# Surplus branches nested, down weights loaded in another order and into two rooms, GpSimd's transfers and subtractions reordered in a routed feed-forward kernel

## The reference

```python
x = x + tanh(g_xattn[0]) * xattn(layernorm(x), ctx, Wq, bq, Wk, bk, Wv, bv)
# xattn: softmax((q Wq + bq)(ctx Wk + bk)^T) / 16 @ (ctx Wv + bv)
x = x + tanh(g_ffn[0]) * ffn(layernorm(x), router_w, gate_w, up_w, down_w)
# ffn: e = argmax(h @ router_w.T) for each token;
#      y = (silu(h @ gate_w[e].T) * (h @ up_w[e].T)) @ down_w[e].T
```

## Time and profile before

| | us |
|---|---|
| median of 3 runs (lowest, highest) | 230.23 (230.07, 230.31) |
| the profiled execution, its own time | 230.14 |
| its span, first to last instruction | 228.3 |
| mean granted TensorE clock | 0.919 of full |

### The profile page before, as it was taken

One profiled execution on the slowest core, in us unless ns is written; L12 is line 12 of the kernel. 1 busy time (PEld: TensorE's weight loads), 2 busy tenths in 40 slices (PEclk: granted clock), 3 DMA queues, 4 the chain that ended last, 5 costly groups with the idle time before them and its releaser, 6 DMA issues.

```text
span 228.3 us, 4589 instructions
## 1 busy us (share of the span) xinstructions
PE 184.3 (81%) x1367; PEld 167.8 (74%) x1367; DVE 109.3 (48%) x366; ACT 109.8 (48%) x251; POOL 135.2 (59%) x143
## 2 busy tenths in 40 slices
PE   7799999997686499979929989966998999996000
PEld 3466899885586299968929988966996999995000
DVE  2488799966597136333305437224355345362000
ACT  2267787765320567856246766527776053140000
POOL 3002269597473897389889479979869940401100
PEclk9999999999587789999997999997999999999555
DMA  6999213947700209321931920691021010100100
GB/s 189 337 388 375 105 48 87 354 137 236 250 0 24 86 4 355 110 84 27 351 114 34 362 90 19 254 355 45 3 59 40 1 50 6 48 4 4 49 9 3
DMA packets 11722, 29.11 MB, mean 127 GB/s; under 512 B 1928, under 2 KB 8537, under 8 KB 10646
## 3 DMA queue, kind: packets, MB, share of 16 engines
q1 hardware_dynamic: 6320, 20.20, 24.9%
q0 software_dynamic: 1920, 4.53, 6.2%
q10 hardware_dynamic: 3430, 3.74, 4.9%
HBM read 24.26 MB, written 4.52 MB: 126 GB/s over the span
## 4 chain that ended last, share of the span: by engine, by line
PE 52%; issue 10%; DMA 10%; POOL 9%; DVE 4%; ACT 4%; ACTq 1%; SPq 1%; POOLq 1%; DVEq 0%
PE ps L1100 19%; PE ps L1132 12%; DMA both<-in_WdL 7%; POOL wgu L490 6%; DMA both<-in_ctxT 4%; PE ps L964 3%; PE ps L903 3%; PE ps L985 3%; PE ps L944 3%; PE ps L933 3%; POOL xin L541 2%; PE ps L974 2%; PE ps L924 2%; POOL out L550 1%; PE ps L1078 1%
## 5 line engine op out<-in xcount | busy, mean ns | idle before, releaser
L1100 PE MATMUL ps<-xhT,wgu 128*128 128x256 f32 (+2 forms) x528 | 74.5, 301 | 12.5 <-ACT V L781 8.7
L1100 PEld LDWEIGHTS ps<-xhT,wgu 128*128 128x128 f32 x528 | 71.1, 200 | 15.2 <-ACT V L781 9.6
L490 POOL TENSOR_TENSOR wgu<-raw_gu,wgu 128x352 fp32r<-128x352 f32 (+1 forms) x28 | 52.7, 1916 | 8.4 <-ACT wgu L678 8.3
L1132 PE MATMUL ps<-wd,hT 128*128 128x256 f32 (+1 forms) x340 | 41.9, 282 | 0.6 <-issue 0.3
L1132 PEld LDWEIGHTS ps<-wd,hT 128*128 128x128 f32 (+1 forms) x340 | 40.4, 180 | 1.1 <-issue 1.1
L550 POOL DMA_INDIRECT out<-xin,table x20 | 19.7, 985 | 34.5 <-DVE xin L1438 30.6
L1416 DVE TENSOR_TENSOR ps<-V,ps 128x256 f32<-128x256 f32 (+2 forms) x40 | 17.8, 446 | 42.8 <-PE ps L1100 28.1
L499 POOL TENSOR_TENSOR wd<-both,wd 128x512 fp32r<-128x512 f32 (+1 forms) x12 | 28.6, 2394 | 0.0
L781 ACT ACTIVATE V<-ps 128x256 f32<-128x256 f32 (+2 forms) x40 | 15.7, 394 | 20.4 <-PE ps L1100 20.1
L541 POOL DMA_INDIRECT xin<-x_rows,table x20 | 19.4, 971 | 9.9 <-issue 9.9
L678 ACT ACTIVATE wgu<-raw_gu 128x704 fp32r<-128x704 f32 (+2 forms) x34 | 24.0, 773 | 1.6 <-issue 1.5
(11 more groups left out here) (146 smaller groups left out, 240.6 us busy)
## 6 DMA issues: line engine op xcount, KB each, us to landing
raw_gu<-in_Wgu SPq DMA_DIRECT2D x8, 1408.0 KB, 6.5
both<-in_Wd SPq DMA_DIRECT2D x8, 640.0 KB, 5.0
x_rows<-x ACTq DMA_DIRECT2D x8, 256.0 KB, 3.5
xin<-in_x SPq DMA_DIRECT2D x7, 256.0 KB, 10.5
both<-in_WdL SPq DMA_DIRECT2D x16, 64.0 KB, 5.3
both<-in_ctxT ACTq DMA_DIRECT2D x2, 480.0 KB, 9.4
xin<-x_rows,table POOLq DMA_INDIRECT x20, 3.0
out<-xin,table POOLq DMA_INDIRECT x20
```

Source lines behind the costliest of these rows:

```text
L490: pool.tensor_tensor(lo[where], raw[where], hi[where].bitcast(F32), ALU.subtract)
L1100: last = pe.matmul(ps[:, bank, 0:n], weights(j, w_part, c, i, kind), xhT[:, j % 2, x_part, c, 0:n], start=(c == 0 and (w_part, x_part) == ...
L1132: last = pe.matmul(y_of(k, size), hT[:, h_part, some], wd[:, j % SPLIT, i, w_part, :], start=(s == 0 and n == 0 and k % 2 == 0), stop=(s = ...
```

## The change

- `surplus` nests the six conditional bodies: body k+1 lies inside body k, so that one branch passes over all of them.
- `split_first` and SP's loads take the down weights of experts 0 to 2 before their gate/up weights; POOL's `low_d` goes ahead of `low_gu` for experts 0 and 1.
- `room_d`: experts 3 to 7 use rooms 0, 1, 0, 1, 0 (before 1, 0, 1, 0, 1). Load d3 waits for `t_stat`, and SP's stream has it ahead of gu4; from then on gu(e), d(e).
- POOL fetches two blocks before it loads the expert's count, and in iteration j it does gather j+2, subtractions of j+2, scatter j-1.
- ACT: `split_d` is cut in two halves, one after the second chunk, one after the fourth; a small Silu ahead of the expert stage; the wait for the sent rows moves from ACT to SP (and to POOL inside the surplus body).
- PE waits for the low part of the third block (`v_xhT3`) only where there is a third block.

```diff
-            for k in range(MORE):
-                with eng.If(n_more > k):
-                    run(E + k)
-                    eng.sem_inc(idle, 1)
+            def turn(k):
+                if k < MORE:
+                    with eng.If(n_more > k):
+                        run(E + k)
+                        turn(k + 1)
+                        eng.sem_inc(idle, 1)
+
+            turn(0)
...
+        def room_d(j):
+
+            return 1 if j < SPLIT else (j + 1) % 2
...
             def load_d(j, of, tail):
-                if j == SPLIT + 1:
+                if j == SPLIT:
 
                     sp.wait_ge(t_stat, 1)
                 elif j:
 
-                    sp.wait_ge(a_hd, j if j <= SPLIT else j - 1)
-                    sp.wait_ge(p_ld, j if j <= SPLIT else j - 1)
-                place = raw_d[:, 1 if j <= SPLIT else j % 2]
+                    sp.wait_ge(a_hd, j if j < SPLIT else j - 1)
+                    sp.wait_ge(p_ld, j if j < SPLIT else j - 1)
+                place = raw_d[:, room_d(j)]
...
+            load_d(0, Wd[0], WdL[0])
             load_gu(0, Wgu[0])
-            load_d(0, Wd[0], WdL[0])
             load_gu(1, Wgu[1])
-            for e in range(1, E):
-                if e + 1 < E:
-                    load_gu(e + 1, Wgu[e + 1])
+            for e in range(1, SPLIT):
                 load_d(e, Wd[e], WdL[e])
+                load_gu(e + 1, Wgu[e + 1])
+            load_d(SPLIT, Wd[SPLIT], WdL[SPLIT])
+            for e in range(SPLIT + 1, E):
+                load_gu(e, Wgu[e])
+                load_d(e, Wd[e], WdL[e])
+            sp.wait_ge(v_used, 1)
+            sizes = [count(sp, j) for j in range(E)]
...
             surplus(sp, "sp", run)
+            for r in (3, 4, 0, 1, 2):
+                sent(r)
...
             for e in range(SPLIT - 1):
+                low_d(e, 3)
                 low_gu(e, 4)
-                low_d(e, 3)
...
                 for k in range(FULL):
                     fetch(j, k, d_gath[r][k])
+                if j == 0:
+                    pool.wait_ge(v_used, 1)
+                sizes.append(count(pool, j))
                 third(pool, "pool", sizes[j], lambda: fetch(j, FULL, d_rest[r]))
...
             for j in range(E):
-                if j:
-                    scatter(j - 1)
                 if j + AHEAD < E:
                     gather(j + AHEAD)
-                    sizes.append(count(pool, j + AHEAD + 1))
                 if SPLIT <= j + AHEAD < E:
                     low_gu(j + AHEAD, 1)
                     low_d(j + AHEAD, 1)
+                if j:
+                    scatter(j - 1)
...
+            act.activation(negc[:, 0:1], negc[:, 0:1], ACT.Silu)
...
                 chunks(j, 0, 2, sizes[j])
-                if j and SPLIT <= j + AHEAD < E:
-                    split_d(j + AHEAD)
+                now = j and SPLIT <= j + AHEAD < E
+                if now:
+                    split_d(j + AHEAD, 0)
...
                     gathered3(j + 1, sizes[j + 1])
+                if now:
+                    split_d(j + AHEAD, 1)
                 chunks(j, 4, CI, sizes[j])
...
-            for r in (3, 4, 0, 1, 2):
-                sent(r)
-            act.sem_inc(a_sent, 1)
...
+                if s == 0 and n > SIZES[0]:
+                    pe.wait_ge(v_xhT3, j + 1)
...
                 pe.wait_ge(v_xhT, j + 1)
-                pe.wait_ge(v_xhT3, j + 1)
```

More of the change, by code:

```diff
@@ L455, in _, with sent, both_of @@
             surplus(sp, "sp", run)
+            def sent(r):
+                def both_of(first):
+                    third(sp, "sp", sizes[r + SEATS], lambda: sp.wait_ge(d_scat[r], 16 * (first + BL)),
+                          lambda: sp.wait_ge(d_scat[r], 16 * (first + FULL)))
+                if r + SEATS < E:
+                    third(sp, "sp", sizes[r], lambda: both_of(BL), lambda: both_of(FULL))
+                else:
+                    third(sp, "sp", sizes[r], lambda: sp.wait_ge(d_scat[r], 16 * BL),
+                          lambda: sp.wait_ge(d_scat[r], 16 * FULL))
+            for r in (3, 4, 0, 1, 2):
+                sent(r)
         @block.gpsimd
@@ L495, in low_d @@
                 pool.wait_ge(a_hd, j + 1)
-                raw = raw_d[:, 1 if j <= SPLIT else j % 2]
+                raw = raw_d[:, room_d(j)]
                 for c in range(0, CI, CI // pieces):
@@ L553, in send, with sent, both_of @@
                     oob_is_err=False).then_inc(signal, 16)
+            def sent(r):
+                def both_of(first):
+                    third(pool, "pool", sizes[r + SEATS], lambda: pool.wait_ge(d_scat[r], 16 * (first + BL)),
+                          lambda: pool.wait_ge(d_scat[r], 16 * (first + FULL)))
+                if r + SEATS < E:
+                    third(pool, "pool", sizes[r], lambda: both_of(BL), lambda: both_of(FULL))
+                else:
+                    third(pool, "pool", sizes[r], lambda: pool.wait_ge(d_scat[r], 16 * BL),
+                          lambda: pool.wait_ge(d_scat[r], 16 * FULL))
             def gather(j):
@@ L569, in scatter @@
                 third(pool, "pool", sizes[j], lambda: send(j, FULL, d_scat[j % SEATS]))
-            pool.wait_ge(v_used, 1)
-            sizes = [count(pool, 0)]
+            sizes = []
             for j in range(AHEAD):
                 gather(j)
-                sizes.append(count(pool, j + 1))
             low_gu(SPLIT - 1, 1)
@@ L596, in run @@
                     pool.wait_ge(v_where, 1)
-                    pool.wait_ge(a_sent, 1)
+                    for r in range(SEATS):
+                        sent(r)
                 if j >= E + SEATS:
@@ L691, in high_d @@
                 some = slice(size * part, size * (part + 1))
-                last = high(raw_d[:, 1 if j <= SPLIT else j % 2, some, :], wd[:, j % SPLIT, some, 0, :])
+                last = high(raw_d[:, room_d(j), some, :], wd[:, j % SPLIT, some, 0, :])
                 if part == parts - 1:
@@ L801, in split_gu, with split_d @@
                     high_gu(j, n, 4)
-            def split_d(j):
-                act.wait_ge(d_d[load_of(j)[0]], 48 * load_of(j)[1])
-                act.wait_ge(t_y, FULL * (j - SPLIT + 1))
-                act.wait_ge(t_y3, j - SPLIT + 1)
-                for n in range(2):
-                    high_d(j, n, 2)
+            def split_d(j, n):
+                if n == 0:
+                    act.wait_ge(d_d[load_of(j)[0]], 48 * load_of(j)[1])
+                    act.wait_ge(t_y, FULL * (j - SPLIT + 1))
+                    act.wait_ge(t_y3, j - SPLIT + 1)
+                high_d(j, n, 2)
             def chunks(j, lo, hi, n_tokens):
@@ L819, in chunks @@
                 sized(act, "act", n_tokens, run)
-            def sent(r):
-                def both_of(first):
-                    third(act, "act", sizes[r + SEATS], lambda: act.wait_ge(d_scat[r], 16 * (first + BL)),
-                          lambda: act.wait_ge(d_scat[r], 16 * (first + FULL)))
-                if r + SEATS < E:
-                    third(act, "act", sizes[r], lambda: both_of(BL), lambda: both_of(FULL))
-                else:
-                    third(act, "act", sizes[r], lambda: act.wait_ge(d_scat[r], 16 * BL),
-                          lambda: act.wait_ge(d_scat[r], 16 * FULL))
+            act.activation(negc[:, 0:1], negc[:, 0:1], ACT.Silu)
             act.wait_ge(v_used, 1)
@@ L837, in _ @@
                 gathered(0, k)
+            turned_x(0)
             gathered3(0, sizes[0])
-            turned_x(0)
             turned_x3(0, sizes[0])
@@ L875, in run @@
                 split_gu(j)
-                split_d(j)
+                split_d(j, 0)
+                split_d(j, 1)
                 chunks(j, 0, CI, None)
```

7 lines of the change are left out of this document (3 added, 4 removed).

## The result

| | before | after |
|---|---|---|
| median of the runs, us (lowest, highest) | 230.27 (230.07, 230.74) | 217.76 (216.61, 220.46) |
| the profiled execution, its own time | 230.14 | 217.28 |
| its span | 228.3 | 215.5 |
| mean granted TensorE clock | 0.919 | 0.936 |

A forecast was written before the change was run, and what follows sets the result against it. PE was taken to set the pace only at the end; before that it waits, and a 19.3 us tail computes nothing. Span 228.3 - 11.4 - 11.5 + 0 + 0.3 = 205.7, so 207.5 us, range 202.5 to 213.

The forecast's parts named there:

- Part 1: Kernel end: nested bodies leave one branch per engine; tail after the last product falls from 19.3 to 7.9 us, -11.4.
- rival C: Kernel end: branch price goes with the code passed over, so the tail keeps 19.3 us; 219 us, chance 0.04.
- Part 2: Experts 1 to 5: earlier down loads remove ACT's weight waits; -17.5 us ideal plus 6 lost, so -11.5 (-15.5 to -7.5).
- 1.2 us lost in each of five experts: Experts 1 to 5: loss left over after the weight waits go, 6 us in all (bounds 2 and 10).
- Theory 2: Expert stage, from the follow-up experiments: ACT's down split in two halves, or other traffic, holds up what ACT gets from PE.
- rival A: Experts 1, 3, 5: the whole loss comes from the unsplit `split_d`, so 6 us shrink to 1 or less; about 202, chance 0.15.
- Rival B: Expert stage: GpSimd's transfers hold up PE, costing 2 us or more in each of five experts; about 213, chance 0.15.
- Part 3: GpSimd in the expert stage: reordered work is done over 10 us before PE needs it; change zero.
- Part 4: Start of the experts: earlier first gather -1.0 us, d3's load slowing the second gather +1.0; together 0 (-1.1 to +2.0).
- Part 5: Attention stage: d2 is issued later and ACT may wait for it near 52 us; +0.3 us (0 to +1.6).
- the edits at zero: Early Silu on ACT and PE's dropped wait for the third block: both taken to cost or gain nothing.

The follow-up runs named there:

- sends_first: The changed kernel with GpSimd's iteration in the old order (scatter j-1, gather j+2, subtractions of j+2): 219.95 us, ratio 0.9588 to the kernel before.
- d3_late: The changed kernel with SP's load of expert 3's down weights held until the first expert's gathers have landed: 213.01 us, ratio 0.9252 to the kernel before.
- d3_again: The same program as d3_late, unchanged, run again in a later sitting with even signals: 201.26 us, ratio 0.8819 to the kernel before.
- spread: The changed kernel with GpSimd's gathers and sends put one by one between pieces of its subtractions: 205.18 us, ratio 0.9048; again 205.03 us, 0.9017.
- d3_spin: d3_late with 72 idle products on PE ahead of the experts instead of 24: 219.01 us, ratio 0.9523 to the kernel before.
- no_sends_3: The changed kernel without the sends of experts 0 to 6, whose rows are not written, in a held sitting: 206.15 us (one run).

## Why the prediction was right and where it was wrong

**Part 1, right.** One branch on PE and a drain on GpSimd that ends last; the source views of lines 320 and 70 of the kernel after, which answer to the earlier trace rows:

```profile
L320 PEldq COMPARE_BRANCH  x1: 3916/3916/3916, 206.8 to 206.8; - x1
```

```profile
L70 ACTq DRAIN  x1: 80/80/80, 207.7 to 207.7; - x1
L70 POOLq DRAIN  x1: 4436/4436/4436, 210.8 to 210.8; - x1
L70 PEldq DRAIN  x1: 73/73/73, 210.8 to 210.8; - x1
...
L70 SPq DRAIN  x1: 13/13/13, 213.7 to 213.7; - x1
```

The tail is 215.5 - 207.9 = 7.6 us for 7.9. SP, with the wait for the sent rows, is done at 213.7, inside GpSimd's drain, which ends at 215.2. A branch past all six bodies costs 3.9 us here and 3.3 to 3.8 in the traces of the other nested kernels, about what one of the short ones costs and far from six times that: rival C is gone. The Trainium skill, "Runtime: NRT & Kernel Launch", section "Instruction fetch mechanics", says that a taken branch whose target lies outside the fetched pages stalls for the fetch of the target's page; one stall of 3.9 us for six bodies agrees.

**Part 2, the pace right, the residual loss wrong.** The chain of waits names no transfer of down weights any more, and PE's pace without waits is what was worked out: 14.7, 12.3, 16.6, 12.4 and 14.8 us are 70.8, for a forecast of 71.9. The step that failed is the term "1.2 us lost in each of five experts". It was formed from the losses of experts 1, 3 and 5 in the kernel before, cut by 0.8 for the halves of the split, and neither the spread nor the count of that held. First, the loss is not even over the experts: 4.1 in expert 3, 2.3 in expert 5, 1.6 in 4, 0.4 in 2 and a gain of 0.4 in expert 1, 8.0 in all for 6. Second, experts 0 and 6 were taken as free because they lost nothing before. They lost nothing because no long run of transfers lay over their up phase: before, a run of two in expert 0 (88.4 to 90.6), and after, one of five, since the scatter of the old order no longer stands between; it cost 5.4 us there and 1.7 in expert 6. sends_first shows the same from the other side: with the old order back, experts 0 and 6 take 14.4 and 14.8 us in a held sitting. The prediction had the sentence that the transfers "now drift over the up phases of experts 3 to 6", and then priced expert 6 at nothing. Of the 9.8 us that were missed, 7.1 are these two experts.

The forecast had named this sign of being wrong itself: ACT waiting for PE in the experts over which the indirect transfers lie. Theory 2, the split, has no run on its side. Expert 6 has no down split and loses 1.7 us held, and in even sittings the halves are there and nothing is lost. So rival A's reason was wrong, and that its time of 202 is near the 203.7 of the even sitting is luck. Rival B's mechanism is the one that the runs bear out, at a higher price than its 213. Rivals A and B were put as two guesses at one fixed state of the chip; the runs show a time near A's and one beyond B's for one program. The range, cut at 213, stopped at B's centre. The sum of the bounds was off as well: the upper ones give 228.3 - 8.1 - 7.5 + 2.0 + 1.6 = 216.3 us of span and so 218.2 of time, not 216.

**Part 3, right in what it said, too narrow in what it asked.** GpSimd binds nowhere in the expert stage. But its order decides over which products its transfers lie, and the forecast asked only when GpSimd would be done. In a held sitting the new order is worth little by itself: experts 0 to 6 take 115.9 us in the changed kernel and 116.1 in sends_first. A run costs where it meets up products that are still to be done. d3_late differs from the changed kernel only in the one load; beside the 2 us at the start it gains 4.6 us in expert 0, whose up products are nearly through when the gathers begin, and gives 1.0 back in expert 1.

**Part 4, taken as zero, and 1.8 us worse than that.** The first gather is issued 0.9 us earlier after the table, as forecast. GpSimd's and ACT's timelines of the kernel after:

```profile
70.26 1.41 POOL L570 DMA_INDIRECT xin<-x_rows,table  x1 [2.71 <-DVE table L1414]
```

```profile
75.16 0.60 ACT L799 ACTIVATE A<-xin,stat 128x256 f32<-128x256 f32 x1 [13.10 <-DMA xin<-x_rows,table]
76.91 0.60 ACT L799 ACTIVATE A<-xin,stat 128x256 f32<-128x256 f32 x1 [1.16 <-DMA xin<-x_rows,table]
```

ACT's second normalization begins 6.65 us after the first gather's issue, and in the kernel before 4.23 (71.77 to 76.00). In d3_late it begins 4.9 us after that issue, so d3's load, issued at 71.36 between the gathers, costs 1.8 us and not 1.0. The first up product then comes 9.8 us after the first gather's issue, for 7.0 before, and for 7.7 and 7.6 in d3_late and d3_again, so that 2.0 of the 2.7 are the load's. The 0.7 that is left stays unexplained, and part of it is scatter: with the old gathers and d3's load after them it takes 7.0 to 7.5 us in four traces. That the transfers of all engines share the same 16 engines, which the Trainium skill says in "DMA: Bandwidth & Descriptors", section "Issuing engines are not separate DMA queues", agrees with these 2 us; the forecast named the mechanism, bounded it at 2.0, and took the middle.

**Part 5 and the edits at zero, right.** ACT waits 0.50 us for d2, ahead of its split at 51.57, where 0.3 was taken. The dropped wait for the third block and the early Silu show no cost.

**What stays open.** What makes a sitting held or even: one chip was both within minutes, and one program ran under both, so neither the program nor the chip alone decides. By which path GpSimd's transfers reach PE is open too; no run separates the issuing of a transfer from its traffic. spread was meant to, and fell twice into an even sitting. It never ran in a held one. Expert 0 took 19.4, 18.2, 15.8 and 14.8 us in four held runs (after, d3_spin, no_sends_3, d3_late) with its five gathers starting 3.5, 5.1, 2.7 and 1.3 us before the end of its last up product; the two longest overlaps cost the most, but their order is the wrong way round, so the overlap alone doesn't settle it.

## What to carry to other kernels

A wait that is removed may have covered another of the same length, so before the gain is booked, ask what else lies over those microseconds, above all a run of indirect transfers on GpSimd, and over which products it will lie afterwards. An engine that is early everywhere still has a price by where it places its transfers. And when several different treatments all give one time, run the untreated kernel again beside them before reading anything into it.

## What the runs showed of the hardware

- Beside five or six indirect transfers in a row, the signals of finished products came up to 4.2 us late in the changed kernel and up to 5.4 in the others, in experts 3, 5 and 6 in a burst 1.1 to 1.3 us after the run's last transfer ended; in another sitting the same program had none over 0.01 us late (217.8 and 203.7 us).
- Beside such a run idle products started 0.7 us apart instead of 60 ns, seen once, in a held sitting.
- One taken branch over six bodies costs PE 3.3 to 3.9 us, and one over a single body 2.9 to 3.5.
- GpSimd's last drain takes 3.6 to 4.9 us in the 20 traces, and it sets the end in the changed kernel, where PE's branches and ACT's wait for the sent rows are gone.
- A load of 770 KB issued between two gathers delays what waits for them by 1.8 to 2.1 us (the changed kernel against the same with d3 late, in the held and in the even sittings).
